# Cross-attention and a mixture-of-experts block on one core: the probabilities' three groups of transposes in a row, and a load issued behind the last of them

## The chip, the cores and the metric

The kernel runs on one core of one Trainium2 chip. The metric is the device time of one execution in microseconds (us). The engines are TensorE (PE in the profile, with its weight loads as PEld), VectorE (DVE), ScalarE (ACT), GpSimd (POOL) and SyncE (SP), which only issues DMAs here. ScalarE issues some DMAs too, from its own queue of instructions (ACTq).

## The reference

For 64 batch elements of 256 tokens with 256 features each:

```python
x = x + xattn(layernorm(x), ctx)      # 8 heads of 64, 77 context rows of 192 features
x = x + ffn(layernorm(x))

# xattn: softmax(q k^T / 8) v, then @ Wo + bo
# ffn: rw = softmax over the experts that the gating lets through (16 experts)
q = sum_e rw[e] * (x @ q_proj[e])     # k and v the same way, 64 wide
attn = causal_softmax(q k^T / 8) v
out  = sum_e (attn * rw[e]) @ o_proj[e]
```

## The kernel before

Each batch element n goes through a first part (layernorm, scores against the context, softmax, product with a matrix made from the context) and a second part (layernorm, gating, the experts' q, k and v, causal attention, the experts' output). Products are made from operands split in two rounded halves, "hi" and "lo": ScalarE rounds a result in PSUM to its hi half, then VectorE subtracts and writes the lo half, and only then is the PSUM bank free. One product is three matmuls (lines 554 to 556).

The program is software-pipelined. A step i works on five elements at once, and every engine has its own order of the step's work, written out by hand in its function `step`; the engines meet only at semaphores. In step i the second part of element i-1 is finished (`before`), that of element i begins (`now`), element i+1 (`ahead`, called `probs_of` where its probabilities are handled) goes through its softmax and product, and element i+2 (`nxt`, or `normed`) through its first layernorm. Steps repeat in a pattern of three, because the jobs that turn the context of three elements at a time into matrices (`turn("E1")`, `turn("E2")`, `turn("E3")`, `turn("M1")` and so on) differ from step to step.

What touches the change:

- `b_qkv(n, j)`, j from 0 to 15, is one of 16 expert blocks: on TensorE two products, six matmuls of 384 columns, into one of three PSUM banks `bank_b`; on VectorE two multiply-adds into `acc` (line 1454), which free the bank. "Block 14" below is j = 13, "block 15" is j = 14, "block 16" is j = 15.
- `a_pT(n, k)`, k = 0, 1, 2 (slots PT0, PT1, PT2), transposes the softmax's probabilities in three groups of 4, 2 and 4 transposes (line 699). ScalarE rounds each group to `pT_hi` (lines 1056 and 1053), VectorE writes `pT_lo` (lines 1400 and 1396).
- The slots share three PSUM banks `bank_a` in the order of `A_ORDER`: ..., E1, E2, PT0, PT1, PT2, E3, M1, XT, M2, ... Each slot waits (`freed`) until the slot three places ahead of it has been read out: PT2 for E2, E3 for PT0, M1 for PT1, XT for PT2, M2 for E3.
- `c_rw(n)` on ScalarE issues two DMAs that bring the routing weights back from DRAM, spread over partitions, into `rw_all` (line 1141), which VectorE needs for `mix` (line 1495) late in the step.
- `ln1_b` on ScalarE (line 1083) writes the normed rows of element i+2 over the tile of the probabilities, and so waits for the third group of transposes. Behind it in ScalarE's queue stand the rounding of E3's result (line 1018 or 1039), that of the second layernorm's transposes `b_xT` (line 1061), of M1's result and of XT (line 960), then `c_qk` (lines 1108 to 1111).

Of the kernel before, what the change touches and what calls it, by code (L numbers as in the profile page):

```python
# [12 lines left out]
def xattn_moe_kernel(nc, x, ctx_in, Wq, Wk, Wv, Wo, bo, sim_matrix, gates, q_proj, k_proj, v_proj, o_proj, out, rw_dram):  # L13
# [65 lines left out]
    def on(n):  # L79
        return 0 <= n < B  # L80

    def job(i, slot):

        if slot not in JOBS[i % 3] or i < -1:
            return None
        kind, f = JOBS[i % 3][slot]
        gm = i // 3 + (2 if kind == "ct" or i % 3 == 2 else 1)
        return (gm, kind, f) if 1 <= gm < GROUPS else None
# [46 lines left out]
    with es:  # L135
# [415 lines left out]
        def _(pe):  # L551
# [92 lines left out]
            def j_k(gm, hc):  # L644
                weights(gm, W_K)
                pe.wait_ge(ct_evac, at(1, gm, 0))
                keys = slice(0, KP)
                context_product(bank_job(gm, "k", hc)[:, keys], wk, slice(hc * P, (hc + 1) * P), keys).then_inc(kv_fill, 1)
# [203 lines left out]
            def step(i):  # L852
                nxt, ahead, now, before, earlier = i + 2, i + 1, i, i - 1, i - 2
                normed, rows, probs_of = [n if n >= start else -1 for n, start in ((nxt, 2), (ahead, 2), (ahead, 1))]

                def do(n, fn, *k):
                    if on(n):
                        fn(n, *k)

                def fill(slot, n, fn, *k):  # L860
                    if on(n):
                        freed(slot, i)
                        fn(n, *k)

                def turn(slot):
                    if job(i, slot):
                        gm, kind, f = job(i, slot)
                        freed(slot, i)
                        if kind == "ct":
                            j_ct(gm)  # L870
                        elif kind == "k":
                            j_k(gm, f)
                        elif kind == "v":
                            j_v(gm, f)
                        elif kind == "g":
                            j_g(gm, f)
                        else:
                            j_u(gm, f)

                do(before, b_qkv, 6)  # L880
                turn("E0")
                do(before, c_rT)
                do(before, b_qkv, 7)
                if i != B:
                    do(earlier, c_y, 0)
                fill("S0", rows, a_s, 0)
                do(before, b_qkv, 8)
                fill("S1", rows, a_s, 1)
                if i != B:
                    do(earlier, c_y, 1)  # L890
                do(before, b_qkv, 9)
                fill("S2", rows, a_s, 2)
                do(before, b_qkv, 10)
                fill("S3", rows, a_s, 3)
                if i != B:
                    do(earlier, c_y, 2)
                do(before, b_qkv, 11)
                turn("E1")
                if i != B:
                    do(earlier, c_y, 3)  # L900
                turn("E2")
                do(before, b_qkv, 12)
                fill("PT0", probs_of, a_pT, 0)
                fill("PT1", probs_of, a_pT, 1)
                do(before, b_qkv, 13)
                fill("PT2", probs_of, a_pT, 2)
                do(before, b_qkv, 14)
                turn("E3")
                do(before, b_qkv, 15)
                do(now, b_xT, 0)  # L910
                do(now, b_xT, 1)
                turn("M1")
                fill("XT", normed, a_xT)
                turn("M2")
                do(before, c_qk)
                if i == B:
                    c_y(B - 2, 0)
                    c_y(B - 2, 1)
                do(now, b_qkv, 0)
                do(now, b_qkv, 1)  # L920
                turn("M3")
                do(now, b_qkv, 2)
                do(before, c_s)
                if i == B:
                    c_y(B - 2, 2)
                    c_y(B - 2, 3)
                fill("Y", ahead, a_y, 0)
                do(ahead, a_y, 1)
                do(before, c_pT)
                turn("L1")  # L930
                do(now, b_qkv, 3)
                do(before, c_pv)
                do(now, b_qkv, 4)
                do(now, b_qkv, 5)
                turn("L2")

            for i in range(-1, B + 2):
                step(i)
# [3 lines left out]
        def _(act):  # L942
# [240 lines left out]
            def step(i):  # L1183
                nxt, ahead, now, before, earlier = i + 2, i + 1, i, i - 1, i - 2
                normed, rows, probs_of = [n if n >= start else -1 for n, start in ((nxt, 2), (ahead, 2), (ahead, 1))]

                def do(n, fn, *k):
                    if on(n):
                        fn(n, *k)

                def turn(slot):
                    if job(i, slot):
                        gm, kind, f = job(i, slot)
                        if kind == "ct":
                            j_ct(gm)
                        elif kind == "k":
                            j_k(gm, f)
                        elif kind == "v":
                            j_v(gm, f)
                        elif kind == "g":  # L1200
                            j_g(gm, f)
                        else:
                            j_u(gm, f)

                turn("E0")
                if i == 0:
                    split_weights(11)
                do(before, c_rT)
                do(rows, a_exp, 0)
                do(rows, a_exp, 1)  # L1210
                do(rows, a_exp, 2)
                do(rows, a_exp, 3)
                do(now, ln2_b)
                turn("E1")
                if i == 0:
                    split_weights(12)
                turn("E2")
                if i == 0:
                    split_weights(13)
                do(probs_of, a_pT, 0)  # L1220
                do(probs_of, a_pT, 1)
                do(before, c_rw)
                do(probs_of, a_pT, 2)
                if i == 0:
                    split_weights(14)
                do(normed, ln1_b)
                turn("E3")
                do(now, b_xT, 0)
                do(now, b_xT, 1)
                turn("M1")  # L1230
                if i == -1:
                    split_weights(8)
                do(normed, a_xT)
                do(before, c_qk)
                turn("M2")
                if i == -1:
                    split_weights(9)
                do(before, c_exp)
                do(now, b_exp)
                turn("M3")  # L1240
                do(now, b_first, 0)
                do(before, c_pT)
                do(now, b_first, 1)
                turn("L1")
                if i == 0:
                    split_weights(15)
                do(before, c_pv)
                do(before, c_mix, 0)
                do(before, c_mix, 1)
                do(before, c_mix, 2)  # L1250
                do(before, c_mix, 3)
                turn("L2")
                if i == -1:
                    split_weights(10)

            for i in range(-1, B + 2):
                step(i)
# [3 lines left out]
        def _(dve):  # L1261
# [11 lines left out]
            def split_weights(k):  # L1273
                dve.wait_ge(wt_hi, k + 1 if k < CC else k + 1 - CC)
                for lo, hi, view in PIECES[k][2]:
                    last = V.tensor_tensor(lo, view(stage[STAGE[k]]), hi.bitcast(F32), ALU.subtract)
                last.then_inc(wt_ready, 1)
# [235 lines left out]
            def step(i):  # L1513
                nxt, ahead, now, before, earlier = i + 2, i + 1, i, i - 1, i - 2
                normed, rows, probs_of = [n if n >= start else -1 for n, start in ((nxt, 2), (ahead, 2), (ahead, 1))]

                def do(n, fn, *k):
                    if on(n):
                        fn(n, *k)
# [41 lines left out]
                turn("E2")  # L1561
                if i == 0:
                    split_weights(13)
                do(probs_of, a_pT, 0)
                do(probs_of, a_pT, 1)
                do(before, b_qkv, 13)
                do(probs_of, a_pT, 2)
                if i == 0:
                    split_weights(14)
# [106 lines left out]
            for i in range(-1, B + 2):  # L1676
                step(i)
# [184 lines left out]
```

## Time and profile before

| | before |
|---|---|
| median of 3 runs | 2558.81 us (2558.7 to 2559.17) |
| the profiled execution | 2557.84 us, its span 2556.0 us |
| busy: PE, PEld, DVE, ACT, POOL | 97%, 95%, 83%, 62%, 43% of the span |
| mean granted TensorE clock | 0.986 of full speed |
| DMA | 441.48 MB, mean 173 GB/s |

The span is the time from the first to the last instruction of the profiled execution; the rest of its 2557.84 us lies around it. Busy shares are averages: TensorE's matmuls overlap, so that what it loses is better seen in the distance from one start to the next. The profiled execution is 0.97 us faster than the median of the runs.

### The profile page before, as it was taken

The page shows a single profiled execution, that of the slowest core. Times are in us where ns is not written, and L with a number is a line of the kernel's source. Part 1 is how long each engine was busy: PE and PEld are TensorE (multiplying, and loading weights), DVE is VectorE, ACT ScalarE, POOL GpSimd, SP SyncE. Part 2 cuts the span into 40 slices and gives each one's busy share as a digit, 9 for nine tenths or more (in the row PEclk, how much of TensorE's full clock was granted, in tenths as well). Part 3 has the DMA queues.
Part 4 walks back from the last instruction along what each step waited for, and adds up shares of the span by engine and source line. Part 5 has one row for each costly group of instructions (what it writes and reads, how often), then busy time and mean ns, then how long its engine had stood idle before and what let it go on. Part 6 is the DMA issues. An engine that isn't in the chain of part 4 may idle for free.

```text
span 2556.0 us, 54410 instructions
## 1 busy us (share of the span) xinstructions
PE 2476.8 (97%) x17308; PEld 2426.4 (95%) x17308; DVE 2124.5 (83%) x6126; ACT 1584.6 (62%) x5126; POOL 1102.1 (43%) x1741
## 2 busy tenths in 40 slices
PE   5699999999999999999999999999999999999997
PEld 4699999999999999999999999999999999999997
DVE  5688888888888888888888888888888888888885
ACT  5566666666666666666666666666666666666642
POOL 2144444444444444444444444444444444444442
PEclk8799999999999999999999999999999999999998
DMA  5655555565555555565565556465565556465531
GB/s 170 212 180 172 185 172 178 157 191 175 180 179 177 178 172 186 151 199 173 173 190 172 171 176 188 148 207 171 165 199 172 164 176 196 143 207 169 165 118 46
DMA packets 288070, 441.48 MB, mean 173 GB/s; under 512 B 20356, under 2 KB 199492, under 8 KB 279723
## 3 DMA queue, kind: packets, MB, share of 16 engines
q1 hardware_dynamic: 218155, 369.84, 44.4%
q10 hardware_dynamic: 69632, 68.17, 10.9%
q8 instruction: 140, 2.29, 0.4%
q14 instruction: 143, 1.17, 0.1%
HBM read 254.86 MB, written 181.83 MB: 171 GB/s over the span
## 4 chain that ended last, share of the span: by engine, by line
PE 81%; DVE 6%; POOL 5%; issue 3%; ACT 3%; DMA 1%; SPq 0%; POOLq 0%; DVEq 0%; ACTq 0%
PE bank_b L554 12%; PE bank_b L555 12%; PE bank_b L556 12%; PE bank_c L554 5%; PE bank_c L555 5%; PE bank_c L556 5%; PE bank_a L555 4%; PE bank_a L554 4%; PE bank_a L556 4%; PE bank_a L699 3%; PE bank_a L663 2%; PE bank_a L675 2%; PE bank_a L664 2%; DVE both L1346 1%; PE bank_a L638 1%
## 5 line engine op out<-in xcount | busy, mean ns | idle before, releaser
L1454 DVE SCALAR_TENSOR_TENSOR acc<-bank_b,rw,acc 128x192 f32<-128x192 f32 x1792 | 654.6, 410 | 109.0 <-PE bank_b L556 106.7
L554 PE MATMUL bank_b<-wqkv_hi,x2T_lo 128*128 128x384 f32 (+1 forms) x2048 | 720.4, 352 | 2.9 <-ACT acc L1076 1.9
L555 PE MATMUL bank_b<-wqkv_lo,x2T_hi 128*128 128x384 f32 (+1 forms) x2048 | 693.8, 339 | 0.0
L556 PE MATMUL bank_b<-wqkv_hi,x2T_hi 128*128 128x384 f32 (+1 forms) x2048 | 690.3, 337 | 0.0
L1798 POOL TENSOR_TENSOR mixs_lo<-mix,mixs_hi 128x512 fp32r<-128x512 f32 x254 | 378.2, 1520 | 165.1 <-ACT mixs_hi L1152 165.1
L1046 ACT ACTIVATE probs<-bank_a,s_max 128x77 f32<-128x77 f32 x1024 | 317.8, 330 | 207.1 <-DVE s_max L1384 207.1
L554 PEld LDWEIGHTS bank_b<-wqkv_hi,x2T_lo 128*128 128x128 f32 x2048 | 386.7, 189 | 5.2 <-ACT acc L1076 2.4
L555 PEld LDWEIGHTS bank_b<-wqkv_lo,x2T_hi 128*128 128x128 f32 x2048 | 387.0, 189 | 0.0
L556 PEld LDWEIGHTS bank_b<-wqkv_hi,x2T_hi 128*128 128x128 f32 x2048 | 385.1, 188 | 0.0
L1152 ACT ACTIVATE mixs_hi<-mix 128x512 fp32r<-128x512 f32 x256 | 159.9, 633 | 208.7 <-DVE mix L1495 208.7
L554 PE MATMUL bank_c<-wo_hi,mixs_lo 128*128 128x256 f32 x1000 | 280.9, 281 | 3.7 <-POOL mixs_lo L1798 3.7
L555 PE MATMUL bank_c<-wo_lo,mixs_hi 128*128 128x256 f32 x1000 | 280.0, 280 | 0.0
L556 PE MATMUL bank_c<-wo_hi,mixs_hi 128*128 128x256 f32 x1000 | 279.8, 280 | 0.0
L1791 POOL TENSOR_TENSOR probs<-probs,p_sum 128x616 f32<-128x616 f32 x128 | 155.9, 1218 | 267.2 <-DVE p_sum L1391 267.2
L1495 DVE TENSOR_TENSOR mix<-rw_all,late_tiles 128x512 f32<-128x512 f32 x256 | 245.8, 1000 | 20.5 <-ACT late_tiles L1146 20.5
L1774 POOL TENSOR_TENSOR mix<-acc 128x192 f32<-128x192 f32 x128 | 75.9, 593 | 377.4 <-DVE acc L1454 377.4
L1717 POOL TENSOR_TENSOR pow_out<-pow_in,expo 128x2 f32<-128x2 f32 (+1 forms) x128 | 111.5, 871 | 239.7 <-DVE pow_in L1304 232.6
L1046 ACT ACTIVATION_READ_ACCUMULATOR probs<-bank_a,s_max 128x1 f32 x1024 | 214.5, 209 | 0.0
L554 PEld LDWEIGHTS bank_c<-wo_hi,mixs_lo 128*128 128x128 f32 x1000 | 189.0, 189 | 3.8 <-issue 3.8
L555 PEld LDWEIGHTS bank_c<-wo_lo,mixs_hi 128*128 128x128 f32 x1000 | 188.9, 189 | 0.0
L556 PEld LDWEIGHTS bank_c<-wo_hi,mixs_hi 128*128 128x128 f32 x1000 | 188.7, 189 | 0.0
L554 PE MATMUL bank_a<-uo,pT_lo 128*128 128x256 f32 (+1 forms) x640 | 180.6, 282 | 0.0
(253 smaller groups left out, 6389.4 us busy)
## 6 DMA issues: line engine op xcount, KB each, us to landing
gq<-g_dram SPq DMA_DIRECT2D x63, 1232.0 KB, 5.6
rw_all<-rw_dram ACTq DMA_DIRECT2D x128, 512.0 KB, 6.9
uo<-u_dram SPq DMA_DIRECT2D x63, 1024.0 KB
g_dram<-draft SPq DMA_DIRECT2D x105, 462.0 KB
u_dram<-draft SPq DMA_DIRECT2D x127, 308.0 KB
g_dram<-mixs_lo SPq DMA_DIRECT2D x63, 462.0 KB
xt<-in_x_dram SPq DMA_DIRECT2D x64, 256.0 KB, 4.7
out_dram<-mix SPq DMA_DIRECT2D x62, 256.0 KB, 3.9
```

The source lines that it names most:

```text
L554: nc.tensor.matmul(dst, lhs[1], rhs[0], start=start, stop=False)
L555: nc.tensor.matmul(dst, lhs[0], rhs[1], start=False, stop=False)
L556: return nc.tensor.matmul(dst, lhs[0], rhs[0], start=False, stop=stop)
L699: last = nc.tensor.transpose(bank_pt(n, k)[0:rows, col * P:(col + 1) * P], probs[:, t, chunk * P:chunk * P + rows], ident[:, :])
L1046: last = nc.scalar.activation(probs[:, t, h * NC:(h + 1) * NC], bank_s(n, j)[:, k * NC:(k + 1) * NC], ACT.Exp, bias=s_max[:, j, k:k + 1], ...
L1152: nc.scalar.activation(mixs[0][:, 2 * j:2 * j + 2, :], mix[:, 2 * j:2 * j + 2, :], copy).then_inc(mix_hi, 1)
L1454: V.scalar_tensor_tensor(acc[:, t, k, :], src, rw[:, t, e:e + 1], acc[:, t, k, :], ALU.mult, ALU.add).then_inc(b_evac, 1)
L1495: V.tensor_tensor(mix[:, 2 * j:2 * j + 2, :], rw_all[:, 2 * j:2 * j + 2, :], aT2[:, :].unsqueeze(1).to_broadcast([P, 2, T]), ALU.mult).the ...
L1717: G.tensor_tensor(dst, src, expo[:, 0:m], ALU.pow).then_inc(ln_pow[k], 1)
L1774: G.tensor_tensor(qkv[:, t, :], acc[:, t, 0, :], acc[:, t, 1, :], ALU.add).then_inc(qkv_ready, 1)
L1791: G.tensor_tensor(part, part, p_sum[:, half, 1, :, :].unsqueeze(3).to_broadcast([P, NT, HB, NC]), ALU.mult).then_inc(p_ready, 1)
L1798: G.tensor_tensor(mixs[1][:, 2 * j:2 * j + 2, :], mix[:, 2 * j:2 * j + 2, :], mixs[0].bitcast(F32)[:, 2 * j:2 * j + 2, :], ALU.subtract).t ...
```

## The change

On TensorE block 14 (`b_qkv`, 13) moves ahead of the first two groups of transposes, so that the three groups stand together behind it. On VectorE the two multiply-adds of block 14 move ahead of the first two `pT_lo` in the same way. On ScalarE the third group's rounding moves ahead of `c_rw`, whose two DMAs so are issued after it. No instruction is added or removed.

```diff
@@ TensorE, step @@
                 turn("E2")
                 do(before, b_qkv, 12)
+                do(before, b_qkv, 13)
                 fill("PT0", probs_of, a_pT, 0)
                 fill("PT1", probs_of, a_pT, 1)
-                do(before, b_qkv, 13)
                 fill("PT2", probs_of, a_pT, 2)
                 do(before, b_qkv, 14)
                 turn("E3")
@@ ScalarE, step @@
                 do(probs_of, a_pT, 0)
                 do(probs_of, a_pT, 1)
+                do(probs_of, a_pT, 2)
                 do(before, c_rw)
-                do(probs_of, a_pT, 2)
                 if i == 0:
                     split_weights(14)
                 do(normed, ln1_b)
@@ VectorE, step @@
                 turn("E2")
                 if i == 0:
                     split_weights(13)
+                do(before, b_qkv, 13)
                 do(probs_of, a_pT, 0)
                 do(probs_of, a_pT, 1)
-                do(before, b_qkv, 13)
                 do(probs_of, a_pT, 2)
```

TensorE's queue before, from the end of block 13: `ident,probs` are the transposes, `bank_b` is an expert block.

```order
L556 MATMUL bank_b<-wqkv_hi,x2T_hi 128x384
L699 MATMUL bank_a<-ident,probs 128x128 x4
L699 MATMUL bank_a<-ident,probs 104x128 x2
L554 MATMUL bank_b<-wqkv_hi,x2T_lo 128x384
L555 MATMUL bank_b<-wqkv_lo,x2T_hi 128x384
L556 MATMUL bank_b<-wqkv_hi,x2T_hi 128x384
```

TensorE's queue of the changed kernel, from the end of block 14:

```order
L556 MATMUL bank_b<-wqkv_hi,x2T_hi 128x384
L699 MATMUL bank_a<-ident,probs 128x128 x4
L699 MATMUL bank_a<-ident,probs 104x128 x2
L699 MATMUL bank_a<-ident,probs 128x128 x4
L554 MATMUL bank_b<-wqkv_hi,x2T_lo 128x384
L555 MATMUL bank_b<-wqkv_lo,x2T_hi 128x384
```

Where three groups of transposes were cut by block 14, ten now stand in a row between blocks 14 and 15.

ScalarE's queue at the same place: `pT_hi` are the three roundings, `rw_all<-rw_dram` the two DMAs of `c_rw`, line 1083 is `ln1_b`, line 1039 E3's rounding.

```order
 L1056 ACTIVATE pT_hi<-bank_a 128x4x128
 L1053 ACTIVATE pT_hi<-bank_a 104x256
-L1141 DMA rw_all<-rw_dram 64x8x256 x2
-L1056 ACTIVATE pT_hi<-bank_a 128x4x128
+L1056 ACTIVATE pT_hi<-bank_a 128x4x128
+L1141 DMA rw_all<-rw_dram 64x8x256 x2
 L1083 ACTIVATE probs<-xt,shift,pow_out 128x256 x2
 L1039 ACTIVATE mixs_lo<-bank_a 116x2x256
```

The DMAs' issue moved from in front of the third rounding to in front of `ln1_b`.

VectorE's queue at the same place: `mixs_lo` is the lo half of E2's result, `acc` are the multiply-adds of the expert blocks.

```order
 L1379 TENSOR_TENSOR mixs_lo<-bank_a,mixs_lo 116x2x256
-L1400 TENSOR_TENSOR pT_lo<-bank_a,pT_hi 128x4x128
-L1396 TENSOR_TENSOR pT_lo<-bank_a,pT_hi 104x256
-L1454 SCALAR_TENSOR_TENSOR acc<-bank_b,rw,acc 128x192 x2
+L1454 SCALAR_TENSOR_TENSOR acc<-bank_b,rw,acc 128x192 x2
+L1400 TENSOR_TENSOR pT_lo<-bank_a,pT_hi 128x4x128
+L1396 TENSOR_TENSOR pT_lo<-bank_a,pT_hi 104x256
 L1400 TENSOR_TENSOR pT_lo<-bank_a,pT_hi 128x4x128
```

Block 14's multiply-adds moved ahead of the first two lo halves of the probabilities.

## Rows read from the trace of the kernel before

**Rows 1.** Windows (start:end, length, busy of PE, PEld, DVE, ACT, POOL, clock, DMA, GB/s)

```profile
1000.00:1500.00 500.00, 497.89 (x3523) 489.27 (x3522) 425.99 (x1230) 317.27 (x1030) 226.19 (x354) 1.00 0.57 177
```

**Rows 2.** Waits of TensorE's weight loads, 500 to 2400 us (us, times, longest)

```profile
PEld bank_a L638 <- DVE mixs_lo L1373: 8.9, 34, 0.3
PEld bank_a L663 <- DVE both L1346: 7.1, 17, 0.7
```

**Rows 3.** Timeline of TensorE in one step around the transposes (start, duration)

```profile
1208.62 0.82 PE L699 MATMUL bank_a<-ident,probs 128*128 128x128 f32 x6
1209.19 0.42 PE L554 MATMUL bank_b<-wqkv_hi,x2T_lo 128*128 128x384 f32 x1
1209.45 0.33 PE L555 MATMUL bank_b<-wqkv_lo,x2T_hi 128*128 128x384 f32 x1
...
1210.33 0.60 PE L699 MATMUL bank_a<-ident,probs 128*128 128x128 f32 x4
1210.69 0.42 PE L554 MATMUL bank_b<-wqkv_hi,x2T_lo 128*128 128x384 f32 x1
...
1211.67 0.33 PE L556 MATMUL bank_b<-wqkv_hi,x2T_hi 128*128 128x384 f32 x1
1211.84 0.27 PE L663 MATMUL bank_a<-both,wq 128*128 128x232 f32 x1
1211.94 0.28 PE L664 MATMUL bank_a<-only,wq 128*128 128x232 f32 x1
```

**Rows 4.** Timeline of ScalarE in the same step (ACTq is a DMA's issue)

```profile
1209.26 0.60 ACT L1056 ACTIVATE pT_hi<-bank_a 128x512 fp32r<-128x512 f32 x1 [0.92 <-PE bank_a L699]
1209.54 0.58 ACTq L1141 DMA_DIRECT2D rw_all<-rw_dram  x1
1209.75 0.38 ACT L1053 ACTIVATE pT_hi<-bank_a 104x256 fp32r<-104x256 f32 x1
1210.14 0.67 ACTq L1141 DMA_DIRECT2D rw_all<-rw_dram  x1
1210.97 0.60 ACT L1056 ACTIVATE pT_hi<-bank_a 128x512 fp32r<-128x512 f32 x1 [0.84 <-PE bank_a L699]
1211.47 1.08 ACT L1083 ACTIVATE probs<-xt,shift,pow_out 128x256 f32<-128x256 f32 x2
1212.48 0.56 ACT L1018 ACTIVATE mixs_lo<-bank_a 128x462 fp32r<-128x462 f32 x1
1213.76 0.66 ACT L1061 ACTIVATE x2T_hi<-bank_b 128x256 fp32r<-128x256 f32 x2 [0.71 <-PE bank_b L736]
...
1215.96 0.38 ACT L1108 ACTIVATE q_rows<-bank_c 64x256 fp32r<-64x256 f32 x1 [0.47 <-PE bank_c L762]
```

**Rows 5.** Timeline of VectorE in the same step

```profile
1209.52 0.63 DVE L1373 TENSOR_TENSOR mixs_lo<-bank_a,mixs_lo 128x462 fp32r<-128x462 f32 x1
1210.07 0.68 DVE L1400 TENSOR_TENSOR pT_lo<-bank_a,pT_hi 128x512 fp32r<-128x512 f32 x1
...
1210.99 0.74 DVE L1454 SCALAR_TENSOR_TENSOR acc<-bank_b,rw,acc 128x192 f32<-128x192 f32 x2
...
1213.53 0.74 DVE L1454 SCALAR_TENSOR_TENSOR acc<-bank_b,rw,acc 128x192 f32<-128x192 f32 x2 [0.55 <-PE bank_b L556]
1214.19 0.63 DVE L1373 TENSOR_TENSOR mixs_lo<-bank_a,mixs_lo 128x462 fp32r<-128x462 f32 x1
```

**Rows 6.** Timeline of TensorE's late weight load for M2, and its matmuls

```profile
1214.87 0.19 PEld L638 LDWEIGHTS bank_a<-cT_hi,wk_lo 128*128 128x128 f32 x1 [0.26 <-DVE mixs_lo L1373]
```

```profile
1215.09 0.27 PE L639 MATMUL bank_a<-cT_lo,wk_hi 128*128 128x232 f32 x1
```

**Rows 7.** The load of the routing weights (issue ns min/median/max, landing), and its first reader

```profile
L1141 ACTq DMA_DIRECT2D rw_all<-rw_dram x128: 581/652/1031, 139.4 to 2525.2; - x128
...
DMA to landing us min/median/max: 4.8/6.9/12.2
```

```profile
L1495 DVE TENSOR_TENSOR mix<-rw_all,late_tiles x12: 685/754/1779, 1226.5 to 1306.3; 128x512 f32<-128x512 f32 x12
```

**Rows 8.** Windows: a stretch near the end at the lower clock

```profile
2512.00:2518.00 6.00, 4.72 (x17) 4.73 (x18) 2.83 (x8) 2.14 (x7) 0.24 (x1) 0.50 0.00 0
```

## Prediction

> **What bounds the kernel now.** I read the page's shares first, then the windows, then who waits for whom, then the timeline of one step engine by engine around the moved instructions. In the windows TensorE is busy for 497.89 of 500 us, at a granted clock of 1.00, its upper level (2.4 GHz) [rows 1]. So only two things can move the time: the distance from one matmul's start to the next, and the few waits that TensorE has left. Its two commonest waits are weight loads that stand late for VectorE: the job in M2 (line 638) for the lo half of E3's result, and the job in L1 (line 663) for the lo half of M2's result [rows 2]. Each is a few tenths of a us in a step. All other engines have slack somewhere, and the question is whether the moved work stays inside it. Both orders of the queues hold from step 1 to step 62 (element i-1 and element i+1 must both exist), so every amount below counts 62 times. A wait is worth 0.2% (5.1 us, about what a measurement of this kernel can tell from no change) only from 0.083 us a step.
>
> **TensorE's own time.** I write times of the step as 8.62 for 1208.62 us. Before: six transposes 8.62 to 9.19 (0.57), block 14 to 10.33 (1.14), four transposes to 10.69 (0.36), block 15 to 11.84 (1.15), together 3.22 [rows 3]. The first matmul behind transposes is followed after 0.26 (9.19 to 9.45), a later one after about 0.175 (block 15's from 11.67 to 11.84 is 0.17), so block 14 without transposes ahead of it costs 1.14 - 0.085 = 1.055. Inside a group the transposes start 0.11 apart (six busy for 0.82, less the 0.27 that the last takes, over five), while the last one is followed after only 0.57 - 0.55 = 0.02 to 0.03. Ten in a row therefore take 9 x 0.109 + 0.03 = 1.01. After: 1.055 + 1.01 + 1.15 = 3.215. The change-over from transposes to matmuls that falls away costs 0.085 and gives back 0.08. I take 0.005 a step as gained, 0.3 us in all; the ends are nothing and 0.085 x 62 = 5.3 us, if the short last distance should not be lost with it.
>
> **The first group's rounding, and who waits for it.** The first transposes move from 8.62 to 9.67. ScalarE began 0.64 after them (9.26) and will at 10.31, until 10.91 [rows 4]. VectorE by then has done E2's lo half (9.52 + 0.63 = 10.15 [rows 5]) and block 14's two multiply-adds (0.74 from about 10.07, so 10.81), and takes the first lo half from 10.94 to 11.62. TensorE's job in E3 needs that bank. Its weight load stands right behind the start of block 15's last matmul: 11.67 before [rows 3], 11.66 after. A weight load followed the releasing instruction by 0.05 in M2 (VectorE 14.19 + 0.63 = 14.82 [rows 5], load at 14.87 [rows 6]), so here it can start at 11.67. And a late one is forgiven a little: in M2 the second matmul started 0.22 after the late load (15.09), in E3 it starts 0.27 after the load's normal place (11.94). Up to 0.05 or 0.06 of lateness costs nothing. I count 0.01 to 0.04 over the three kinds of step, so nothing is lost, but this is the thinnest cover in the change: 0.03 thicker than needed.
>
> **The third group.** Its transposes start at 9.67 + 6 x 0.109 = 10.33, where they stood before, since block 14 lies ahead of them in both orders. E2's bank is free at 10.15, as before. Its transposes end no later, but ScalarE, busy with the first two groups, takes it at 10.31 + 0.49 + 0.28 = 11.08 instead of 10.97, until 11.68. VectorE then ends the third lo half at about 12.55 and block 15's multiply-adds at 13.20. Before, it stood idle for 0.55 ahead of 13.53 [rows 5], that is from 12.98: this comes 0.2 later and still ahead of block 16's at 13.53, which wait for TensorE. E3's lo half (14.19) and with it the wait in M2 stay where they are. POOL's sum of the first `acc` comes 0.2 later, ahead of the second one, which hangs on block 16 and sets when it ends.
>
> **The DMAs' issue.** It costs the queue of ScalarE 9.54 to 10.81 now, and lies beside the rounding: the first issue starts at 9.54, while the ACTIVATE of 9.26 still runs for 0.32 [rows 4]. Before, it delays nothing, because the third group comes only at 10.97. After, it starts when the third rounding is handed over, at 10.97 + 0.06, and takes the same 1.27: 12.30. `ln1_b` stands behind it and starts at about 12.37 in place of 11.47, 0.90 later. E3's rounding moves from 12.48 to 13.38 (until 13.94, needed by VectorE at 14.19), and the engine takes the next one 0.46 after, at 13.84 in place of 13.76: the 0.71 of idle time in front of line 1061 swallows all but 0.08. The next 0.47 of idle time, in front of `c_qk`, swallows the 0.08. XT on TensorE needs `ln1_b`, now ready at about 13.45, and stands behind the transposes that ScalarE reads only at 13.76. So 0. The load itself lands 1.5 us later: issue at about 11.7 plus 6.9, at worst 12.2, is 18.6 to 23.9; its reader starts at 26.5 [rows 7].
>
> The Trainium skill says the same in "Perfetto Trace Analysis", section "DVE / Act Engine Instruction" and "DMA Instruction — HWDGE": the sequencer hands a compute instruction to a queue and goes on, and a DMA's profiled window is the sequencer's own work. The trace agrees (9.54 lies inside the ACTIVATE of 9.26). If instead the issue had to wait for the third rounding's end at 11.68, `ln1_b` would start at 13.0, E3's rounding would end at 14.57, and VectorE would take it 0.38 late: 24 us in all.
>
> **Sum.** -0.3 + 0 + 0 + 0 = -0.3 us. Against the profiled execution's own 2557.84 us that is 2557.5; the median of the runs stands 0.97 above it, at 2558.81, and gives 2558.5 us.
>
> **Rivals.**
>
> *E3's weight load comes late (slower).* The rounding of the first group now has 2.0 us from its transposes to E3, against 3.05 before. If anything in that chain (ScalarE 0.60, VectorE 0.68, two hand-overs) is over 0.03 later than worked out, TensorE pays the rest in each step. For: VectorE's queue is full in this stretch, so that block 14's multiply-adds, now ahead of the first lo half, leave it only 0.1 us early for it (10.81 against 10.94). Against: the durations repeat within 0.01. At 0.11 late it would be 0.08 a step and count as slower; at 0.15 it is 62 x 0.12 = 7.4 us, 2566 us. The far bound is a whole instruction of 0.33, 62 x 0.3 = 19 us. Chance 0.06.
>
> *The delay of ScalarE passes on to `c_qk` (slower).* From `c_qk` runs the chain that ends in TensorE's wait in L1. It takes another 0.25 us of delay before VectorE feels it in E3's lo half. The second issue took up to 1.03 instead of 0.67 [rows 7], 0.36 more, so a step with such an issue loses 0.1; were it all of them, 6 us: 2565 us. Such issues are rare in the trace (the median is 0.652). Chance 0.03.
>
> *The clock drops (slower).* Ten transposes in a row are the longest run of them in a step. Near the end of the program the granted clock is 0.50 in one stretch, its lower level (1.2 GHz) [rows 8], and at half the clock the same columns take twice the time. Against: six in a row leave it at 1.00 in every step [rows 1]. If it fell only from the transposes to the end of block 15, that would be 2.2 us more a step, 134 us, 2693 us. Chance 0.01.
> The Trainium skill speaks against the change here: "TensorE: Matmul & The Clock Gate", section "Part 4: PE-mode transpose", names transposes as work under which the full clock does not engage. By that rule a longer run of them is a risk; the trace, with 1.00 over 500 us that hold six in a row in every step, shows none.
>
> *A change-over less is worth its whole 0.085 (faster).* Then the last of each group's short distance is kept and the time falls by 5.3 us, to 2553.5 us. For: the gap behind transposes is in every step. Against: the two halves of it cancel in these rows. Chance 0.05, all of it just at the border.
>
> **How the numbers follow.** The forecast, cover holds, has 0.85 and its own range 2557.3 to 2560. The rivals have 0.15. To the other side I reach to half of the first rival's price, for small late loads of 0.03 to 0.06 a step (2 to 4 us), and below for part of a change-over: 2556 to 2562.5 us. Faster by over 0.2%: 0.05. Slower: 0.06 + 0.03 + 0.01 = 0.10. The rest, 0.85, within 0.2%.
>
> **What would show it.** In the profile after, ten transposes start 0.109 apart and block 14 takes 1.055; the load of line 663 or 675 in E3 stands within 0.05 of the last matmul of block 15 and has no wait of its own in the list of waits; line 1083 starts about 0.9 later against the transposes, but lines 1061 and 1108 still wait for TensorE. A new entry "PEld bank_a L663 (or L675) <- DVE pT_lo L1400" would make the forecast wrong, and so would an idle time of nothing in front of line 1108, or a clock below 1.00 in the middle of the program.

## The result and the profile after

| | before | after |
|---|---|---|
| median of 4 runs | 2558.86 us (2558.7 to 2559.17) | 2577.09 us (2574.45 to 2578.71) |
| the profiled execution, its span | 2557.84, 2556.0 us | 2576.28, 2574.5 us |

The changed kernel takes 1.0068 of the time before (95% interval 1.0056 to 1.0080): 18.2 us more, slower, where no change was forecast and the range ended at 2562.5.

The windows of the changed kernel, in the columns and the stretch of [rows 1]:

```profile
1000.00:1500.00 500.00, 495.09 (x3501) 486.42 (x3500) 423.71 (x1226) 312.39 (x1027) 223.44 (x352) 1.00 0.58 176
```

The clock is still 1.00, but TensorE is busy 2.8 us less and makes 22 of 3523 matmuls fewer in the same 500 us, 0.6%: the loss lies in the steps, not in the clock. The list of TensorE's waits of the changed kernel (matmuls, 500 to 2400 us: us, times, longest) says where:

```profile
PE bank_a L638 <- DVE mixs_lo L1379: 6.5, 16, 0.5
PE bank_a L622 <- ACT probs L1083: 3.7, 8, 0.7
PE bank_a L663 <- DVE both L1346: 3.4, 17, 0.4
PE bank_a L675 <- DVE both L1346: 3.0, 16, 0.4
```

and that of its weight loads, to be laid beside [rows 2]:

```profile
PEld bank_a L638 <- DVE mixs_lo L1379: 10.3, 16, 0.7
PEld bank_a L638 <- DVE mixs_lo L1373: 10.1, 33, 0.6
PEld bank_a L663 <- DVE both L1346: 7.4, 17, 0.6
...
PEld bank_a L622 <- issue: 5.5, 9, 0.9
```

The kernel before has one more entry of line 638 than [rows 2] shows, from the other kind of E3 job:

```profile
PEld bank_a L638 <- DVE mixs_lo L1379: 4.7, 16, 0.3
```

The wait that the prediction was afraid of, E3's weight load for line 1400, is not there. What has grown is the job in M2 (line 638), which waits for the lo half of E3's result (4.7 to 10.3 us and 8.9 to 10.1), and new is XT (line 622), which waits for `ln1_b` (line 1083). Both hang on what stands behind the two DMAs in ScalarE's queue. The DMAs' own line in the changed kernel (issue ns min/median/max):

```profile
L1141 ACTq DMA_DIRECT2D rw_all<-rw_dram x128: 581/654/2588, 139.6 to 2542.5; - x128
```

Its median is that of [rows 7], 654 against 652, but the longest is 2588 instead of 1031. A median over 128 issues hides what happens to some twenty of them. ScalarE's timeline in a step that goes as forecast:

```profile
795.30 0.60 ACT L1056 ACTIVATE pT_hi<-bank_a 128x512 fp32r<-128x512 f32 x1
795.32 1.27 ACTq L1141 DMA_DIRECT2D rw_all<-rw_dram  x2
796.71 1.09 ACT L1083 ACTIVATE probs<-xt,shift,pow_out 128x256 f32<-128x256 f32 x2 [0.81 <-issue]
797.71 0.54 ACT L1018 ACTIVATE mixs_lo<-bank_a 128x462 fp32r<-128x462 f32 x1
798.15 0.64 ACT L1061 ACTIVATE x2T_hi<-bank_b 128x256 fp32r<-128x256 f32 x2
...
800.25 0.38 ACT L1108 ACTIVATE q_rows<-bank_c 64x256 fp32r<-64x256 f32 x1 [0.46 <-PE bank_c L762]
```

and TensorE in the same step:

```profile
793.90 1.31 PE L699 MATMUL bank_a<-ident,probs 128*128 128x128 f32 x10
794.98 0.42 PE L554 MATMUL bank_b<-wqkv_hi,x2T_lo 128*128 128x384 f32 x1
...
796.11 0.27 PE L663 MATMUL bank_a<-both,wq 128*128 128x232 f32 x1
```

Ten transposes stand in a row, block 15 follows, E3 starts 2.21 us behind the first transpose (2.16 forecast), the two issues take 1.27 together, line 1061 has lost its idle time and line 1108 still has 0.46 of it. Now a step that is lost, 270 us later:

```profile
1064.76 0.61 ACTq L1141 DMA_DIRECT2D rw_all<-rw_dram  x1
1064.80 0.60 ACT L1056 ACTIVATE pT_hi<-bank_a 128x512 fp32r<-128x512 f32 x1
1065.40 2.05 ACTq L1141 DMA_DIRECT2D rw_all<-rw_dram  x1
1067.57 1.09 ACT L1083 ACTIVATE probs<-xt,shift,pow_out 128x256 f32<-128x256 f32 x2 [2.17 <-issue]
1068.57 0.58 ACT L1039 ACTIVATE mixs_lo<-bank_a 116x512 fp32r<-116x512 f32 x1
1069.05 0.64 ACT L1061 ACTIVATE x2T_hi<-bank_b 128x256 fp32r<-128x256 f32 x2
```

The first issue is as ever, the second takes 2.05 instead of 0.66 us. "2.17 <-issue" in front of line 1083 says that ScalarE waited for nothing but its own queue. The chain of waits of this stretch carries it on to TensorE:

```profile
1065.40 2.04 ACTq L1141
1067.44 0.04 issue
...
1068.08 0.59 ACT probs L1083
1068.66 0.49 ACT mixs_lo L1039
1069.15 0.02 issue
1069.18 0.70 DVE mixs_lo L1379
1069.88 0.04 issue
1069.92 0.38 PE bank_a L638
```

The step is 39.75 us long where such a step took 38.48.

**Which steps.** I went through the trace of both kernels step by step (steps 2 to 60; the length of a step is the distance of its first transpose to that of the next one). Three kinds of step follow each other, by what SP stores at this place, which is the result of the E2 job: two stores where it is a job of `u` (line 434); one store of another kind (line 420); and none.

| kind of step | second issue of `c_rw`, mean (longest): before | after | step length: before | after |
|---|---|---|---|---|
| two `u` stores (19 steps) | 0.68 (0.96) | 1.39 (2.05) | 38.48 | 39.12 |
| one other store (20) | 0.70 (1.03) | 0.79 (0.96) | 38.05 | 38.09 |
| no store (20) | 0.66 (0.66) | 0.73 (1.59) | 38.10 | 38.18 |

The first issue took 0.58 to 0.61 us in every one of these steps of both kernels. The steps' difference is 19 x 0.64 + 20 x 0.04 + 20 x 0.09 = 14.8 of the span's 18.5 us; the rest lies in steps outside the count, most of all in step 1, which has the issue of 2588 ns. Over the 18 steps with `u` stores whose second issue took more than 1.0, a line through step length against issue has a slope of 1.04 and meets the old 38.48 at 0.76: the room was 0.1 us, and every tenth beyond it is paid in full. Two steps without a store at this place had a long second issue as well, step 21 with 1.59 us and step 48 with 1.24; they make up most of what that row lost.

What is different in the stores is when they come. SP's timeline before, and below it after, both in the kind of step with `u` stores (the first transposes at 826.29 and 1063.41):

```profile
824.92 0.71 SPq L434 DMA_DIRECT2D u_dram<-draft  x2
825.71 0.71 SPq L468 DMA_DIRECT2D out_dram<-mix  x1
827.86 0.68 SPq L434 DMA_DIRECT2D u_dram<-mixs_lo  x2
```

```profile
1060.97 0.71 SPq L434 DMA_DIRECT2D u_dram<-draft  x2
1062.02 0.81 SPq L468 DMA_DIRECT2D out_dram<-mix  x1
1063.90 0.71 SPq L434 DMA_DIRECT2D u_dram<-mixs_lo  x2
```

In such a step E1's job is one of `u` too: its two stores (from `draft`) come first, then the output's (line 468), then E2's two (from `mixs_lo`), which are the ones meant below. In before the second issue of `c_rw` starts at 827.83, 0.03 ahead of E2's stores, and 2.6 to 2.9 us behind E1's, and is not stretched. After, it starts 1.50 us behind the first of E2's stores. The stores keep their place against E2; the transposes, and with them the load, have moved about 1.07 us later against them, and the load another 0.44 against the transposes.

### The profile page after: what moved, and what is told of

It is laid out like the page before. It is cut to its first block, busy times and chain, and to the rows that moved or that the text cites. A ratio compares the mean times of both kernels' runs of the same rounds, so it can differ in the third digit from the quotient of the medians.

```text
span 2574.5 us, 54410 instructions
## 1 busy us (share of the span) xinstructions
PE 2484.5 (97%) x17308; PEld 2433.5 (95%) x17308; DVE 2129.4 (83%) x6126; ACT 1569.6 (61%) x5126; POOL 1105.0 (43%) x1741
## 3 DMA queue, kind: packets, MB, share of 16 engines
q14 instruction: 143, 1.17, 0.1%
## 4 chain that ended last, share of the span: by engine, by line
PE 77%; DVE 6%; POOL 5%; ACT 5%; issue 4%; ACTq 2%; DMA 1%; SPq 0%; POOLq 0%; DVEq 0%
PE bank_b L554 12%; PE bank_b L555 11%; PE bank_b L556 11%; PE bank_c L554 5%; PE bank_c L555 5%; PE bank_c L556 5%; PE bank_a L554 4%; PE bank_a L555 4%; PE bank_a L556 4%; PE bank_a L699 2%; ACTq L1141 2%; PE bank_a L663 2%; PE bank_a L675 1%; DVE both L1346 1%; PE bank_a L664 1%
```

## The experiments

Each ratio is to runs of the kernel before on the same chip, with its 95% interval.

### One half of the change alone

`e1_pe_dve_only` keeps the new order of TensorE and VectorE, and puts ScalarE's back.

```diff
 # ScalarE, on the changed kernel
                 do(probs_of, a_pT, 1)
-                do(probs_of, a_pT, 2)
                 do(before, c_rw)
+                do(probs_of, a_pT, 2)
```

> Changed kernel with ScalarE's order of before (the two DMAs in front of the third rounding), TensorE and VectorE as changed. Theory (the second issue of the routing weights' load is slow where SP has just issued the u stores, and what stands behind it on ScalarE comes late): the second issue now falls about 1.56 us after the first transposes in place of 1.98, still behind the u stores (0.5 and 0.77), so it stays over 1 us in one step of three, and the third rounding and line 1083 wait for it: 2565 to 2578 us. Rival (the move on ScalarE alone is to blame, TensorE's and VectorE's new order is harmless): 2558 to 2560 us. Rival (late release of E3's bank by the new order on TensorE and VectorE): as slow as the changed kernel, 2577, with waits of line 663 or 675 for pT_lo.

Measured: 2607.62 us, 1.0195 (1.0178 to 1.0212). Its waits of TensorE's matmuls (500 to 2400 us):

```profile
PE bank_b L736 <- DVE acc L1454: 32.2, 47, 2.2
```

This is a worse kernel than either; the theory had named the direction but not the size (2565 to 2578). With all ten transposes in a row the third group is there before the issues are over, so its rounding stands behind them; VectorE's lo half waits for it, block 15's multiply-adds stand behind that, and the transposes of the second layernorm (line 736) wait for their bank, up to 2.2 us at a time. So the two halves of the change need each other: with the transposes together, the rounding has to be ahead of the load. Most of the loss is the slow issue again. The load stands at its old place, 0.91 us behind the first transposes, but these now come later against SP's stores, and the second issue takes 1.67 us on average where E2's `u` stores stand 0.8 to 1.0 us ahead of it. The steps are longer than before by 1.52 us there, by 0.60 with one other store (issue 0.99), and by 0.22 with none (issue 0.66), so about 0.2 us a step is what the order costs by itself.

`e2_act_only` is the other half: the kernel before, with the third rounding ahead of `c_rw`.

> Kernel before with ScalarE's order of the change alone (third rounding in front of the two DMAs). Theory: the issues fall at 2.4 and 3.0 us after the first transposes, the u stores at 1.57 and 1.84, the same distance as in the changed kernel, so the second issue is 1.0 to 2.0 us long in one step of three and the time is that of the changed kernel, 2572 to 2580 us. Rival (TensorE's ten transposes in a row or VectorE's order cost the time): 2558 to 2560 us.

Measured: 2575.44 us (2570.85 to 2575.88), 1.0066 (1.0049 to 1.0082), the changed kernel's 1.0068 within the interval. Its waits of weight loads:

```profile
PEld bank_a L638 <- DVE mixs_lo L1373: 10.3, 33, 0.6
PEld bank_a L638 <- DVE mixs_lo L1379: 9.5, 16, 0.7
...
PEld bank_a L622 <- issue: 2.9, 5, 0.8
```

The same entries as in the changed kernel have grown. One line moved on ScalarE is enough for the whole loss.

### The load out of the way

`e3_load_behind_ln1` is the changed kernel with `c_rw` behind `ln1_b`; `e4_before_load_behind_ln1` is the same edit on the kernel before; `e7_second_dma_behind_ln1` is the changed kernel with the first DMA in its place and only the second behind `ln1_b`.

```diff
 # e3, ScalarE
                 do(probs_of, a_pT, 2)
-                do(before, c_rw)
                 if i == 0:
                     split_weights(14)
                 do(normed, ln1_b)
+                do(before, c_rw)
```

> Changed kernel with the two DMAs one place further back on ScalarE, behind ln1_b (line 1083). Theory: the second issue stays just as slow in one step of three (1.0 to 2.0 us), but line 1083 no longer waits for it, and E3's rounding has 0.9 us more room: 2558 to 2562 us, with waits of line 622 for line 1083 gone. Rival (the load's traffic or its late landing costs the time, not what stands behind the issue): as the changed kernel, 2574 to 2579 us.

> Kernel before with the two DMAs behind ln1_b on ScalarE; TensorE and VectorE as before. Theory (the place of the DMAs' issue decides, the transposes in a row are worth nothing): the same time as the changed kernel with the load behind ln1_b, 2558 to 2561 us, though the second issue is slow in one step of three. Rival (the three groups in a row gain or cost something that the earlier run hid): more than 3 us away from 2559.3.

> Changed kernel with only the second of the two DMAs behind ln1_b; the first stays in front of it. Theory (the second issue alone is the one that grows beside the u stores, the first stays at 0.6): line 1083 starts about 2.1 us after the first transposes, 2558 to 2562 us. Rival (any issue at this place grows): the first is over 0.8 us in one step of three and the time over 2565 us.

Measured: e3 2559.26 us, 1.0005 (0.9995 to 1.0014); e4 2561.73 us, 1.0005 (0.9996 to 1.0014); e7 2561.53 us, 1.0008 (0.9998 to 1.0017). The load's line and the waits of weight loads of e3:

```profile
L1141 ACTq DMA_DIRECT2D rw_all<-rw_dram x128: 581/631/2404, 141.7 to 2526.7; - x128
```

```profile
PEld bank_a L638 <- DVE mixs_lo L1373: 8.7, 33, 0.3
...
PEld bank_a L638 <- DVE mixs_lo L1379: 5.0, 16, 0.6
```

In e3 the second issue is still slow (up to 2404 ns, 1.17 on average in steps with `u` stores), and the time is that of before: line 622 is gone from the list and line 638 is back at its old amounts (8.7 and 5.0 us, 8.9 and 4.7 before). A slow issue costs nothing where what stands behind it has room. Here that is E3's rounding: the issue runs beside `ln1_b` on the engine, and the rounding starts 3.1 to 4.1 us behind the first transposes in steps with `u` stores, against 3.86 before and up to 5.25 in the changed kernel. e3 against e4 is the change of TensorE and VectorE alone, with the load harmless in both: 1.0005 and 1.0005, so ten transposes in a row are worth nothing that these runs can tell, some 3 us either way. e7 shows that the first issue has no part in it: it stays at 0.58 to 0.61 us in front of `ln1_b`. e4's median is 0.7 us above its range; the others lie in theirs.

### Why the issue is slow

`e5_u_stores_behind_load` is the changed kernel with SP's `u` stores held back until `ln1_b` is done, which stands behind both issues.

```diff
 # SP, ahead of the two stores of an E1 job of u
+        if gm and f == 2 and on(step_of(gm, "u", f) + 2):
+            sp.wait_ge(ln_done[0], at(NT, step_of(gm, "u", f) + 2, NT - 1))
```

> Changed kernel, all work kept; in the one step of three whose E1 job is a u job SP waits for ln1_b (line 1083) before it issues the u stores, so that they come behind the load's two issues. Theory: the second issue is back at 0.65 to 0.75 us in those steps, line 1083 starts 2.8 us after the first transposes everywhere, and the time is 2558 to 2562 us (up to 2 us for stores that come late). Rival (the issue is slow for another reason than the stores in front of it, for instance the place on ScalarE): the second issue stays at 1.0 to 2.0 us and the time at 2574 to 2579 us.

Measured: 2572.01 us (2568.88 to 2574.30), 1.0048 (1.0031 to 1.0064), outside both ranges. The second issue in steps with `u` stores fell to 0.68 us on average, from 1.39. But a new entry stands in the waits of ScalarE and one in those of TensorE (the kernel's lines are two further down):

```profile
ACT mixs_lo L1105 <- DMA u_dram<-mixs_lo: 15.4, 15, 2.7
```

```profile
PE bank_c L556 <- DVE mixs_lo L1462: 10.4, 13, 2.4
```

The stores now read their tile so late that ScalarE, which writes it next, waits for them. The cause of the slow issue was hit, and the time went to another place.

The edit reaches further than its name. SP issues in order, so holding back E1's stores holds back what follows them too:

```profile
1065.97 0.71 SPq L436 DMA_DIRECT2D u_dram<-draft  x2
1066.73 0.67 SPq L470 DMA_DIRECT2D out_dram<-mix  x1
```

E1's two stores, the output's store and E2's two all come behind the load here (its second issue starts at 1064.01). So e5 shows that these stores together stretch the issue; it doesn't tell E2's from the others. The long issues of steps 21 and 48 stay (1.39 and 1.41 us), and three with one other store are over 1.0, up to 1.82: the `u` stores are not the only cause of a long issue, and what the other is stays open.

`e6_long_rows` tests another reason: that the load has too many pieces. The routing weights are stored in DRAM in two halves, so that each partition reads one row of 8 KB per DMA.

```diff
 # ScalarE, the store of the routing weights
-                nc.scalar.dma_start(rw_dram[:, :], rwT[:, :]).then_inc(rwT_out, 16)
+                nc.scalar.dma_start(rw_dram[:, :].rearrange("(k a) t -> a k t", k=2), rwT[:, :]).then_inc(rwT_out, 16)
 # ScalarE, c_rw
-                    nc.scalar.dma_start(rw_all[k * D:(k + 1) * D, :, :],
-                                        rw_dram[:, :].rearrange("(a k) t -> k a t", k=2)[k].partition_broadcast(D)).then_inc(rw_all_in, 16)
+                    nc.scalar.dma_start(rw_all[k * D:(k + 1) * D, :, :].rearrange("p a t -> p (a t)"),
+                                        rw_dram[:, :].rearrange("(k a) t -> k (a t)", k=2)[k].partition_broadcast(D)).then_inc(rw_all_in, 16)
```

> Changed kernel, the routing weights laid out in DRAM so that a partition reads 8 KB in one piece in place of eight rows of 1 KB; the same bytes, one eighth of the pieces. Theory (the issue is slow because it writes 512 descriptors while the u stores' traffic runs): both issues fall well below 0.58 us, the second stays below 0.5 in every step, line 1083 starts within 2.4 us of the first transposes, 2557 to 2561 us. Rival (an issue takes its time whatever the number of pieces): second issue 1.0 to 2.0 us in one step of three, 2574 to 2579 us.

Measured: 2571.05 us (2569.03 to 2572.42), 1.0046 (1.0030 to 1.0061). Its load:

```profile
L1141 ACTq DMA_DIRECT2D rw_all<-rw_dram x128: 456/561/1792, 141.6 to 2535.8; - x128
```

The first issue falls from 0.60 to 0.47 us, the second stays at 1.27 on average in steps with `u` stores. The number of the load's pieces is not what stretches it. The time lies between those of before and after, and its interval just meets the changed kernel's (1.0056 to 1.0080).

`e12_u_stores_right_behind` holds the `u` stores back only until ScalarE has issued the load, by a semaphore of their own that ScalarE raises behind the second issue.

```diff
 # ScalarE, at the end of c_rw
+            act.sem_inc(issued, 1)
 # SP, ahead of the two stores of an E1 job of u
+        if gm and f == 2:
+            sp.wait_ge(issued, step_of(gm, "u", f))
```

> Changed kernel, all work kept, a cleaner form of the run with the u stores held back: ScalarE raises a semaphore behind the load's two issues, and SP waits for it (not for ln1_b, which comes 1.3 us later) before the u stores of the E1 job. Theory: second issue 0.65 to 0.70 us in those steps, line 1083 at 2.8 us after the first transposes, and less of ScalarE's waiting for the E2 store than the 15 us of the earlier run, so that the total shows the recovery: 2558 to 2566 us. Rival (the held-back stores cost as much as the slow issue did): 2568 to 2576 us.

Measured: 2573.47 us (2566.22 to 2578.20), 1.0064 (1.0047 to 1.0080). In its profiled execution, the fastest of its runs with 2566.22 us, the second issue was at 0.69 again, and the stores' own price was half of that in e5:

```profile
ACT mixs_lo L1105 <- DMA u_dram<-mixs_lo: 7.1, 13, 1.5
```

For the issue that confirms e5 in a second way, and it too holds back the whole of SP's queue from E1's stores on. Its total settles no price for the cause: the four runs spread over 12 us, as wide as what it should tell apart, and the median lies in the rival's range. The steps of its profiled execution say more. Those with `u` stores are 38.71 us long on average, with a median of 38.49, against 39.12 in the changed kernel and 38.48 before, so in that execution most of their loss is back with the short issue. No trace shows its slower runs.

### What the stretch is worth otherwise

The waits in M2 and L1 were there before the change ([rows 2]), and four kernels go for them. `e8_c_qk_ahead_of_m2` is e3 with TensorE's transposes of `c_qk` ahead of M2, `e9_c_qk_ahead_alone` is that move on the kernel before; `e10_e3_lo_ahead_of_block16` is the kernel before with VectorE's lo half of E3 ahead of block 16's multiply-adds; `e11_both_moves` has the moves of e9 and e10.

```diff
 # e10, VectorE, on the kernel before
                 do(before, b_qkv, 14)
+                turn("E3")
                 do(before, b_qkv, 15)
-                turn("E3")
```

> The changed kernel with the load behind ln1_b, and on TensorE c_qk moved ahead of the M2 job, for a version that beats both. From the chain of the kernel before: TensorE waits 0.26 us for E3's lo half ahead of M2, and 0.3 us ahead of L1 for a chain that begins with c_qk. c_qk can stand 0.4 us earlier, so the chain ends 0.15 to 0.4 earlier (bounded by block 2 on TensorE): 0.1 to 0.3 us a step, 2540 to 2553 us. Rival (c_qk then waits for POOL's second sum in TensorE's queue as long as M2 did, and the chain is bound by block 2): 2557 to 2560 us.

> Kernel before with c_qk ahead of the M2 job on TensorE alone (ScalarE, VectorE and the transposes as before). If the gain of 0.16% of the earlier run came from c_qk's place and none from the change: 2553 to 2557 us beside 2558 to 2560 of the kernel before, with the waits of lines 638, 663 and 675 gone and one of line 762 for POOL's second sum (line 1774) of 0.6 us a step. If the change's order of TensorE and VectorE had a share in it: 2557 to 2560 us.

> Kernel before with E3's lo half ahead of block 16's multiply-adds on VectorE. It takes the idle 0.55 us in front of block 16 and ends about 0.15 us past it, so TensorE's wait in front of M2 (0.26 us a step) goes; block 16, POOL's second sum and c_qk's release come 0.15 later, which c_qk, 0.6 us behind that release now, does not feel. The chain that ends in L1 starts up to 0.26 us earlier, bounded by block 2. 0.15 to 0.3 us a step: 2540 to 2550 us. Rival (the gain is handed to the wait in L1, which grows by what M2's lost, since the chain is bound elsewhere): 2557 to 2560 us.

> Kernel before with both moves: c_qk ahead of M2 on TensorE, and E3's lo half ahead of block 16 on VectorE. c_qk then waits 0.15 us longer for POOL's second sum than with its own move alone, so this is the slower of the combinations by 0.1 to 0.2 us a step: 2557 to 2566 us. If the wait in front of c_qk is hidden after all: below both single moves, 2540 to 2550 us.

Measured: e8 2555.88 us, 0.9984 (0.9975 to 0.9993); e9 2554.53 us, 0.9984 (0.9975 to 0.9993); e10 2541.91 us (2540.33 to 2543.23), 0.9937 (0.9924 to 0.9951); e11 2562.77 us, 1.0017 (1.0008 to 1.0026). e8 and e9 gain the same, so what is gained is the place of `c_qk`, and nothing of it comes from the change. e8 lies between its two ranges, and e9, e10 and e11 in one of theirs. e8 gained less than expected: it and e9 trade the waits of M2 and L1 for one of `c_qk` itself, as the matmuls' waits of e9 show (0.23 us at a time, where 0.6 was expected):

```profile
PE bank_c L762 <- POOL mix L1774: 11.7, 50, 0.3
```

e10 is the best kernel of all, 17 us faster than before and 35 faster than the changed one. VectorE's timeline in e10:

```profile
1205.10 0.73 DVE L1454 SCALAR_TENSOR_TENSOR acc<-bank_b,rw,acc 128x192 f32<-128x192 f32 x2
1205.90 0.64 DVE L1373 TENSOR_TENSOR mixs_lo<-bank_a,mixs_lo 128x462 fp32r<-128x462 f32 x1
1206.46 0.73 DVE L1454 SCALAR_TENSOR_TENSOR acc<-bank_b,rw,acc 128x192 f32<-128x192 f32 x2
```

and its weight loads in M2:

```profile
1207.29 0.14 PEld L622 LDWEIGHTS bank_a<-ident,probs 128*128 128x128 f32 x1
1207.40 0.19 PEld L638 LDWEIGHTS bank_a<-cT_hi,wk_lo 128*128 128x128 f32 x1
```

The lo half fills the idle time in front of block 16 ([rows 5] has 0.55 there), and the load of line 638, 0.26 late in [rows 6], follows 0.11 behind its neighbour. Line 638 is no longer in e10's list of waits at all. e11 adds e9's move to it and loses what both gave, with the wait for line 1774 grown to 17.5 us in 49 times, 0.36 us each: as was expected of it, block 16's multiply-adds now stand behind E3's lo half, so `c_qk` gets its input later, and ahead of M2 nothing covers that.

## Why the prediction was wrong, point by point

**The step that failed** is a term in "The DMAs' issue": the issue moves "and takes the same 1.27". It is a term mis-sized, and it is nearly the whole loss. The two issues took 0.60 + 0.66 at their old place. At the new one the second takes 1.39 on average in one step of three, up to 2.05 in the steps counted. e2 shows that this one move makes the whole difference, e3 and e7 that it does so only through what stands behind the second issue, and the steps whose second issue stays at 0.66 keep their length, but for one (step 42, 0.39 us longer, with `ln1_b` 0.42 behind the issue). I read the duration where the load stood and carried it to where it went, without asking what SP's queue issues there: the stores of line 434 stand in the same trace of before, 0.03 us behind the second issue, and I had no row of SP at all. That the second issue could take 1.03 I had seen in [rows 7], and took for a rare case.

**The room** was the second thing. I counted 0.25 us before VectorE feels `ln1_b` late. The steps show 0.1. Where the issue is short, `ln1_b` starts 0.12 to 0.13 behind its end, where I had taken 0.06 to 0.07, and line 1083 stands at 2.80 behind the first transposes instead of 2.70. With a room of 0.25 the 19 steps would have lost about 19 x (0.73 - 0.25), 9 us by this estimate, instead of 12, so this is the smaller error.

**The rival that named it** was the second, "the delay of ScalarE passes on to `c_qk`", priced at 2565 us if every issue took 1.03. It had the queue and the issue that delays, and failed in two things. Its chance, 0.03, rested on "such issues are rare in the trace", a frequency of the old place. And its place was not `c_qk`: the delay reached TensorE earlier, through `ln1_b` in XT and E3's lo half in M2, as the chain of waits shows.

**What held.** TensorE's own time: 2.13 to 2.21 us from the first transpose to E3 against 2.16, and e3 against e4 puts the regrouping at nothing. The first group's rounding, the thinnest cover by my count: its load in E3 has no entry in the list of waits. The third group: no new wait from it. The issue starts under the third rounding (795.32 inside the ACTIVATE of 795.30) as forecast. The clock stayed at 1.00 with ten transposes in a row, so the third rival has fallen, and no part of the fourth was seen. Line 1061 lost its idle time and line 1108 kept 0.46, both as written, in the undisturbed steps.

**What stays open** is why the stores stretch the issue, which of them does, and what stretched it in the two steps without one. That SP's stores of such a step do is shown by e5 and e12, each of which moved them and got 0.68 and 0.69 back. It isn't the other queue's issue at the same time, since SP's two were over 0.79 us before the slow one began (1063.90 + 0.71 against 1065.40), and by e6 not the number of the load's own pieces. The Trainium skill, "Perfetto Trace Analysis", section "DMA Instruction — HWDGE (DVE, Sync)", lets the profiled window of an issue hold the wait for a shared unit that writes descriptors and names a buffer that can fill; that the stores' descriptors still stood in it would be one reading, but no run here shows it, and e6 does not favour it: there the load has an eighth of the pieces and its second issue is stretched as before. A run with stores of fewer, longer rows would have been the test, and was not made.

## What to carry to other kernels

An issue of a DMA has no fixed duration that moves with it: read what other queues issue in the 1.5 us ahead of the place it goes to, and look at the longest of its kind, not at the median alone. Put a DMA's issue where what stands behind it in the queue has room for the longest one; behind `ln1_b`, beside which it ran, the same slow issue was free. And where a late weight load is the commonest wait, look for idle time on the engine it waits for just ahead of the instruction that is late: e10 is one line moved, and gave 0.63%.

## What the runs showed of the hardware

- In the changed kernel a DMA of the same form took 0.58 to 0.61 us to issue as the first of a pair and 0.65 to 2.05 us as the second (2.59 at the start of the program). The second took 0.95 to 2.05 us where two `u` stores to DRAM from SP's queue had been issued 1.2 to 1.5 us ahead of it, and a single store of line 420 at the same distance did little (0.79 on average). It is not the only cause: in steps 21 and 48, with the nearest store 3.8 us ahead, the second issue took 1.59 and 1.24 us, and both steps are long in e2 to e7 as well (1.05 to 1.72). The Trainium skill, "DMA: Bandwidth & Descriptors", section "Issuing engines are not separate DMA queues", calls the sequencer's time for an issue usually small relative to the DMA. Here the median was 0.654 us against 6.8 from issue to landing, but 2.05 where it was stretched, and that was enough to set the time of a kernel with 0.1 us of room.
- In the changed kernel ScalarE's next instruction, `ln1_b`, started 0.12 to 0.13 us behind the end of the second issue in 56 of the 59 steps counted, and 0.42 us behind it in the other three.
- Rows of 8 KB instead of the shorter pieces shortened an undisturbed issue from 0.60 to 0.47 us.
